# A third buffer, other slots, and ScalarE's two cross blocks moved by DMAs from its own queue

## The reference: what is computed

```python
C_q = Q @ Wq_d
C_kv = K @ Wkv_d
CqWqk = (C_q @ W_qk).reshape(b, n, H, LKV)
scores = jnp.einsum('bnhl,bkl->bhnk', CqWqk, C_kv) / jnp.sqrt(LKV)
attn = jax.nn.softmax(scores, axis=-1)
V_up = (C_kv @ Wv_u).reshape(b, nkv, H, HD)
out = jnp.einsum('bhnk,bkhd->bnhd', attn, V_up)
```

## Time and profile before

| | |
|---|---|
| median of the runs | 2763.66 us |
| the profiled execution, as timed | 2762.25 us |
| its span, first to last instruction | 2760.3 us |
| mean granted clock of TensorE | 0.985 |
| PE busy | 2608.9 us, 95% |
| DVE busy | 2311.5 us, 84% |
| POOL busy | 1938.7 us, 70% |
| ACT busy | 1687.2 us, 61% |
| blocks `b_pt<-b_tn` by DMA | 1152 of 80.0 KB, 2.8 us to landing |

### The profile page before, as it was taken

The page is one execution under the profiler, slowest core; times in us unless marked ns, Lnnn a source line. Parts: engine busy times, 40 slices in busy tenths (PEclk is TensorE's granted clock), DMA queues, the critical chain, the costliest instruction groups (busy, mean ns, idle before and its releaser), DMA issues. The chain is left out here.

```text
span 2760.3 us, 41974 instructions
## 1 busy us (share of the span) xinstructions
PE 2608.9 (95%) x14328; PEld 1983.6 (72%) x14328; DVE 2311.5 (84%) x2664; ACT 1687.2 (61%) x2636; POOL 1938.7 (70%) x1423
## 2 busy tenths in 40 slices
PE   7998899999998999999977999999999999999997
PEld 4665667666666666666656888888888888788885
DVE  2665689889998988788966999999998899899988
ACT  3454687877887778777856544445555555545553
POOL 1002377677777777677766888888887888888883
PEclk9899999999999999999998999999999999999999
DMA  7426677677778676886681222222223222232221
GB/s 274 161 96 203 213 228 216 188 231 212 224 207 260 203 212 197 250 262 207 188 280 69 84 92 100 77 72 74 69 69 130 77 84 77 69 115 77 84 93 76
DMA packets 166791, 420.63 MB, mean 152 GB/s; under 512 B 30130, under 2 KB 57652, under 8 KB 166068
## 3 DMA queue, kind: packets, MB, share of 16 engines
q1 hardware_dynamic: 164276, 409.57, 47.2%
q10 hardware_dynamic: 2304, 8.39, 0.7%
HBM read 248.43 MB, written 75.04 MB: 117 GB/s over the span
## 5 line engine op out<-in xcount | busy, mean ns | idle before, releaser
L1717 DVE SCALAR_TENSOR_TENSOR c_acc<-c_ps,c_sd,c_acc 128x1024 f32<-128x1024 f32 x448 | 573.2, 1282 | 94.6 <-PE c_ps L1564 94.4
L1622 ACT ACTIVATE c_scaled<-c_ps,c_sgu 128x1024 f32<-128x1024 f32 x336 | 375.5, 1117 | 420.7 <-PE c_ps L1564 418.8
L1294 POOL COPY b_pt<-b_tn 32x640 f32<-32x640 f32 x640 | 456.7, 714 | 240.7 <-DVE b_tn L1193 208.2
L1095 ACT ACTIVATE b_pr<-b_sc,b_nm 128x799 f32<-128x799 f32 (+1 forms) x512 | 476.3, 932 | 167.1 <-DVE b_pr L1186 154.6
L1804 POOL TENSOR_TENSOR c_sum_u<-c_sum_u,c_scaled 128x1024 f32<-128x1024 f32 x168 | 404.6, 2408 | 110.5 <-ACT c_scaled L1622 110.2
L1804 POOL TENSOR_TENSOR c_sum_g<-c_sum_g,c_scaled 128x1024 f32<-128x1024 f32 x168 | 404.8, 2410 | 81.9 <-ACT c_scaled L1622 81.6
L1032 PE MATMUL b_po<-b_pt,shared 128*64 128x256 f32 x2560 | 393.1, 395 | 45.9 <-DMA b_pt<-b_tn 44.0
L1013 PE MATMUL b_sc<-b_kh,b_qs 128*128 128x402 f32 (+1 forms) x1024 | 395.3, 386 | 19.8 <-ACT b_pr L1095 15.4
L1193 DVE STREAM_TRANSPOSE b_tn<-b_pr 128x1280 f32<-128x1280 f32 x256 | 385.5, 1506 | 12.2 <-ACT b_pr L1095 6.3
L1013 PE MATMUL b_sc<-b_kl,b_qs 128*128 128x402 f32 (+1 forms) x1024 | 356.8, 348 | 0.0
L1032 PEld LDWEIGHTS b_po<-b_pt,shared 128*64 128x64 f32 x2560 | 197.2, 138 | 196.8 <-DMA b_pt<-b_tn 70.5
(11 more groups left out here) (198 smaller groups left out, 4413.5 us busy)
## 6 DMA issues: line engine op xcount, KB each, us to landing
b_pt<-b_tn SPq DMA_DIRECT2D x1152, 80.0 KB, 2.8
c_uw_int<-wint_u SPq DMA_DIRECT2D x56, 512.0 KB, 3.5
c_gw_int<-wint_g SPq DMA_DIRECT2D x56, 512.0 KB, 3.4
c_dw_int<-wint_d SPq DMA_DIRECT2D x56, 512.0 KB, 3.5
a_cx<-in_b_ctxT SPq DMA_DIRECT2D x16, 1608.0 KB, 10.1
b_rw<-in_c_gw SPq DMA_DIRECT2D x28, 512.0 KB, 4.2
b_rz<-in_c_gz SPq DMA_DIRECT2D x28, 512.0 KB, 5.6
b_rw<-in_c_uw SPq DMA_DIRECT2D x28, 512.0 KB, 4.2
```

The lines of the kernel that those rows point to most:

```text
L1095: S.activation(pr[u % 2][:, k0:k1], sc[:, at + lo:at + hi], ACT.Exp, bias=nm[:, u % 2:u % 2 + 1], accum_out=den[:, g % 2, q, half:half + 1 ...
L1294: G.tensor_copy(pt[s][32 * c:32 * c + 32, a, :, :], tn[s][32 * a:32 * a + 32, c, :, :]).then_inc(s_block, 1)
L1622: S.activation(dst[:, :], pair[SLOT[x, t] % 4][:, :], ACT.Identity, scale=scale(x, t)).then_inc(s_e, 1)
L1717: V.scalar_tensor_tensor(out=total, in0=pair[SLOT[x, t] % 4][:, :], scalar=scale(x, t), in1=total, op0=ALU.mult, op1=ALU.add).then_inc(s_a ...
```

## The change

ACT no longer copies its two groups. It begins a DMA for each from its own queue, one in step 2p+3 and one in step 2p+4, at the end of the step; the semaphore counts DMA landings. `b_pt` gets a third buffer, in the tail of the `shared` tile, so writers wait for the weighing of pair p-3. PE weighs one step later. DVE turns before it projects and before it takes a head's output. ACT exponentiates before it casts projected queries, and copies a head's latent sum (L1116) after the first half's exponent.

As the FFN's buffers lie over `shared`, only two weight tiles are loaded early; four others follow at the end of the attention. In the FFN ACT no longer copies x into `c_acc`: the first down product is added to `c_xh`, and POOL adds `c_xl` to the sum later, once for each of the eight blocks, in the weight tiles 2, 4, ... 16.

```diff
-CN_AT = {27: (1, 0), 35: (1, 1), 75: (2, 0), 83: (2, 1), 139: (3, 0), 147: (3, 1)}
+CN_AT = {28: (1, 0), 36: (1, 1), 76: (2, 0), 84: (2, 1), 140: (3, 0), 148: (3, 1)}
-WEIGH_AT = 5
-OUT_AT = 10
+WEIGH_AT = 6
+LATENT_AT = 9
+OUT_AT = 11
+MOVES = 3
@@ attention: buffers, moved, exchange (SP)
+        pt.append(shared[:, NXC + 2 * NSZ - 8 * SEG:NXC + 2 * NSZ].rearrange("p (a z e) -> p a z e", a=4, z=2))
-            eng.wait_ge(s_cross, len(BY_SCALAR) * (p + 1))
+            eng.wait_ge(s_cross[p % 2], len(BY_SCALAR) * 16 * (p // 2 + 1))
-                if p >= 2:
-                    Q.wait_ge(s_pv, p - 1)
+                if p >= MOVES:
+                    Q.wait_ge(s_pv, p - MOVES + 1)
@@ attention: scalar
-            def cross(p):
+            def cross(p, n):
                 s = p % 2
-                S.wait_ge(s_tt, 2 * p + 2)
-                if p >= 2:
-                    S.wait_ge(s_pv, p - 1)
-                for a, c in BY_SCALAR:
-                    S.copy(pt[s][32 * c:32 * c + 32, a, :, :], tn[s][32 * a:32 * a + 32, c, :, :]).then_inc(s_cross, 1)
+                a, c = BY_SCALAR[n]
+                if n == 0:
+                    S.wait_ge(s_tt, 2 * p + 2)
+                    if p >= MOVES:
+                        S.wait_ge(s_pv, p - MOVES + 1)
+                S.dma_start(pt[p % MOVES][32 * c:32 * c + 32, a, :, :].rearrange("p t e -> p (t e)"),
+                            tn[s][32 * a:32 * a + 32, c, :, :].rearrange("p t e -> p (t e)")).then_inc(s_cross[s], 16)
             for k in range(NU + OUT_AT):
+                if k < NU:
+                    exponent(k, 1)
                 if k % 8 == 5 and k + 3 < NU:
                     project((k + 3) // 4)
-                if k < NU:
-                    exponent(k, 1)
-                if k % 4 == 0 and 8 <= k < NU + 8:
-                    out_latent(k // 4 - 2)
...
                 if k < NU:
                     exponent(k, 0)
+                if k % 4 == LATENT_AT % 4 and LATENT_AT <= k < NU + LATENT_AT:
+                    out_latent((k - LATENT_AT) // 4)
...
-                if k % 2 and 3 <= k < 2 * PAIRS + 3:
-                    cross((k - 3) // 2)
+                if 3 <= k < 2 * PAIRS + 3:
+                    cross(*divmod(k - 3, 2))
@@ attention: vector
+                if 1 <= k <= NU:
+                    turn(k - 1)
                 if k % 8 == 5 and k + 3 < NU:
                     project((k + 3) // 4)
...
-                if 1 <= k <= NU:
-                    turn(k - 1)
@@ ffn
-FIRST = [("u", 0), ("g", 0), ("u", 1), ("g", 1), ("d", 0)]
+FIRST = [("u", 0), ("g", 0)]
+SECOND = [("u", 1), ("g", 1), ("d", 0), ("d", 1)]
+LOW_AT = [2 + 2 * k for k in range(KC)]
@@ ffn: sync
-            load("d", 1)
+            for n, t in SECOND:
+                load(n, t)
@@ ffn: scalar
                 S.copy(xh[:, k, :], ps[:, :]).then_inc(s_xh, 1)
-                if f == 0:
-                    S.copy(acc[:, k, :], ps[:, :]).then_inc(s_init, 1)
@@ ffn: vector
-                total = acc[:, k, :] if n == "d" else part[n][t % 2][:, :]
+                total = before = acc[:, k, :] if n == "d" else part[n][t % 2][:, :]
                 if n == "d":
-                    if t % NI:
+                    if t == 0:
+                        V.wait_ge(s_xh, k + 1)
+                        before = xh[:, k, :].bitcast(F32)
+                    elif t == NI:
+                        V.wait_ge(s_init, KC + k + 1)
+                    elif t == LOW_AT[k] + 1:
+                        V.wait_ge(s_init, k + 1)
+                    else:
                         V.wait_ge(s_a[n], (t - 1) * KC + k + 1)
@@ ffn: gpsimd
+            def add_low(k):
+                G.wait_ge(s_a["d"], LOW_AT[k] * KC + k + 1)
+                G.wait_ge(s_xl, k + 1)
+                G.tensor_tensor(acc[:, k, :], acc[:, k, :], xl[:, k, :].bitcast(F32), ALU.add).then_inc(s_init, 1)
```

More of the change, by code:

```diff
@@ L838, in attention @@
         s_part = sem("nm_part")
-        s_move, s_block, s_cross = [sem("move0"), sem("move1")], sem("block"), sem("cross")
+        s_move, s_block, s_cross = [sem("move0"), sem("move1")], sem("block"), [sem("cross0"), sem("cross1")]
         s_tr, s_pe = sem("tr"), sem("pe")
@@ L902, in exchange @@
                 Q.wait_ge(s_tt, 2 * p + 2)
-                if p >= 2:
-                    Q.wait_ge(s_pv, p - 1)
+                if p >= MOVES:
+                    Q.wait_ge(s_pv, p - MOVES + 1)
                 for a, c in BY_DMA:
-                    Q.dma_start(pt[s][32 * c:32 * c + 32, a, :, :].rearrange("p t e -> p (t e)"),
+                    Q.dma_start(pt[p % MOVES][32 * c:32 * c + 32, a, :, :].rearrange("p t e -> p (t e)"),
                                 tn[s][32 * a:32 * a + 32, c, :, :].rearrange("p t e -> p (t e)")).then_inc(s_move[s], 16)
@@ L1028, in weigh @@
                     if t < NDT:
-                        turned = pt[s][:, :, :, 32 * t:32 * t + 32].rearrange("p a z e -> p z a e")
+                        turned = pt[p % MOVES][:, :, :, 32 * t:32 * t + 32].rearrange("p a z e -> p z a e")
                     else:
@@ L1290, in blocks @@
                 G.wait_ge(s_tt, 2 * p + 2)
-                if p >= 2:
-                    G.wait_ge(s_pv, p - 1)
+                if p >= MOVES:
+                    G.wait_ge(s_pv, p - MOVES + 1)
                 for n, (a, c) in enumerate(BY_POOL):
-                    G.tensor_copy(pt[s][32 * c:32 * c + 32, a, :, :], tn[s][32 * a:32 * a + 32, c, :, :]).then_inc(s_block, 1)
+                    G.tensor_copy(pt[p % MOVES][32 * c:32 * c + 32, a, :, :], tn[s][32 * a:32 * a + 32, c, :, :]).then_inc(s_block, 1)
                     G.wait_ge(s_block, len(BY_POOL) * p + n + 1)
@@ L1428, in ffn @@
         d1 = sb("c_dw_int1", [P, HID], F32R)
-        w = {n: [sb(f"c_{n}w_int{j}", [P, HID], F32R) for j in range(2)] for n in "gu"}
+        w = {"g": [sb("c_gw_int0", [P, HID], F32R)], "u": [sb("c_uw_int0", [P, HID], F32R)]}
+        for n in "gu":
+            w[n].append(sb(f"c_{n}w_int1", [P, HID], F32R))
         w["d"] = [sb("c_dw_int0", [P, HID], F32R), d1]
@@ L1450, in consumed @@
                 eng.wait_ge(s_xl, e[1] * KC + e[2] + 1)
-                if e[1] == 0:
-                    eng.wait_ge(s_init, e[2] + 1)
             elif e[0] == "r":
@@ L1501, in early @@
                 n = p - LATE
-                if 2 <= n < 7:
+                if 2 <= n < 2 + len(FIRST):
                     load(*FIRST[n - 2])
@@ L1716, in accumulate @@
                 V.wait_ge(s_p[n], t * KC + k + 1)
-                V.scalar_tensor_tensor(out=total, in0=pair[SLOT[x, t] % 4][:, :], scalar=scale(x, t), in1=total,
+                V.scalar_tensor_tensor(out=total, in0=pair[SLOT[x, t] % 4][:, :], scalar=scale(x, t), in1=before,
                                        op0=ALU.mult, op1=ALU.add).then_inc(s_a[n], 1)
@@ L1721, in low_turned @@
                 V.wait_ge(s_xh, f * KC + k + 1)
-                if f == 0:
-                    V.wait_ge(s_init, k + 1)
                 V.tensor_tensor(xl[:, k, :], ps[:, :], xh[:, k, :].bitcast(F32), ALU.subtract).then_inc(s_xl, 1)
@@ L1820, in low @@
                 G.tensor_tensor(hl[t % 2][:, :], h[:, :], hh[t % 2][:, :].bitcast(F32), ALU.subtract).then_inc(s_hl, 1)
+            def add_low(k):
+                G.wait_ge(s_a["d"], LOW_AT[k] * KC + k + 1)
+                G.wait_ge(s_xl, k + 1)
+                G.tensor_tensor(acc[:, k, :], acc[:, k, :], xl[:, k, :].bitcast(F32), ALU.add).then_inc(s_init, 1)
             for p, e in walk():
                 if len(e) == 2:
+                    if e[0][0] == "d" and LOW_AT[int(e[0][1])] == e[1]:
+                        add_low(int(e[0][1]))
                     if e[0] == "u0" and 0 <= p - 2 < NT2:
```

2 lines of the change are left out of this document (removed).

## The result

The changed kernel takes 2966.83 us (median of four runs, 2964.20 to 2968.39) where the kernel before takes 2762.26 beside it: 1.0723 times, 95% interval 1.0703 to 1.0743. Five executions of the experiments' kernels took far longer than the others; the ratios and intervals leave them out, the medians in us include them. The forecast was 2735, with 2795 as the far end. The last turning begins at 1636.9 us, before at 1431.7; that is 205.2 us later, and the whole span grew by 205.1 (2760.3 to 2965.4). So the feed-forward part neither won nor lost, and the attention, which now lasts to about 1640, lost everything.

What follows compares the result with a forecast made beforehand. PE (94% busy) and DVE (87%) were taken to bound the attention, so only their waits could be won. Terms -57 + 25 + 5 + 3 + 2 - 6 + 1 = -27 us gave 2735 from 2762.25; range 2685 to 2795.

Steps and rivals of the forecast that it cites:

- ACT's two blocks: DMAs replacing ACT's copies in the attention: no gain counted, 5 us lost for landings above the median; bounds 0 and 90.
- Order of the slots: DVE's projection and output behind its turning: covered by 4.31 us a step, no cost; ACT's latent sum behind an exponent: 2.
- The latent sum: ACT's latent sum behind an exponent, asked for by the next pair's weighing: 0 to 70 us over 64 heads, taken as 2.
- one of the prediction's own signs of being wrong: In the attention, PE stands at `b_po` for ACT's latent sum in more than a few heads; no size given.
- Later weighing and the third buffer: Attention: PE's wait for moved blocks goes, -57 us; DVE inherits 25 of it before its turning, between 8 and 70.5.
- Start of the FFN: ACT loses 8 copies and PE's wait for `c_xl` goes: gain 0 to 8.4 us, taken as 6.
- POOL's adds: Eight adds in the FFN, 19.3 us, fit into POOL's gaps: cost 1 us, ends 0 and 19.3.
- Traffic: 256 more DMAs of 80 KB, 21 MB or 8% more in the attention, lengthen landings: 0 to 8 us, taken as 3.
- A: Slower: ACT's queue begins the second DMA only when the exponent before it has ended; 2818 us, chance 0.14.
- its sign: DVE waits at L1193 in nearly every second unit for 0.4 us or more.
- B: No change: ACT's two issues draw out SP's nine by 0.7 us a pair; 2755 to 2774, say 2765; chance 0.25.
- B's sign: SP's issue of a block takes above 0.65 us, from 0.59.

Runs made afterwards that it cites:

- the late DMA alone: Kernel of 2753 us with only the second DMA of a pair put back behind both exponents of the even step: 2836.38 us, ratio 1.0274.
- the late reads alone: Kernel of 2753 us with only DVE's reads of projection, output and turned latent put back behind its turning: 2802.83 us, ratio 1.0137.
- every late place undone: Changed kernel with DVE's reads, ACT's cast and latent sum early again; both DMAs in the odd step: 2753.18 us (0.9951), or copies instead: 2756.46 (0.9962).
- the kernel of 2753 us: Changed kernel with both DMAs in the odd step, DVE's reads ahead of its turning, ACT's projection cast and latent sum early: 2753.18 us, ratio 0.9951.

## Why the prediction was wrong, step by step

**ACT's two blocks (+5 us): failed, the largest.** The prediction had the second DMA begin 0.64 us after the step's first exponent and land 2.0 to 2.8 later, just in time for a turning that DVE cannot want sooner than 3.50 after that exponent. The step that failed is the landing: 2.0 to 2.8 is what SP's blocks take, and the median landing was taken as what this DMA meets. With the late DMA alone it begins sooner than forecast, at 0.13, and lands 4.5 later, 5.3 beside weight transfers; DVE is ready at 3.96. The term was worth 3.2% (about 89 us) by itself, at the upper bound of 90 that the text gave it.

The program has SP issue a pair's nine blocks ahead of its weight load; what ACT begins comes later, and among the weight transfers. In the changed kernel the second DMA begins 9.7 us after the pair's turning ended (median) and meets one of these transfers in 78 of 126 pairs, two or more in 66.

In the changed kernel the begin is late as well: 1.18 us after the exponent (median of 126 pairs), held by the wait of ACT's copy, with whose start it coincides within 0.05 us in 106 of them. It lands 3.5 after that (median), so some 5.0 after the exponent (median), and DVE is ready at 4.1. The prediction read the queue from one step, in which that copy stood behind no wait that showed:

```profile
730.08 0.47 ACT L1102 COPY b_pe<-b_mi 128x384 f32<-128x384 f32 x1
```

**Order of the slots (nothing): failed.** The cover named, "wanted two steps later", looked at who wants DVE's results. It left out what DVE's reading frees. PE stands in order at its turning until the bank is read; by itself this costs 1.9%, about 51 us, with 31 waits for the projection of 1.5 us and 55 for the output of 0.4:

```profile
PE b_mi L1045 <- DVE b_qs L1176: 48.2, 31, 5.3
...
PE b_mi L1045 <- DVE b_yo L1208: 23.6, 55, 2.7
```

(from the run with the late reads alone). ACT's cast behind its exponent, which the prediction did not price either, costs 32 us where the reads are early. The latent sum, taken at 2 of a possible 70, made PE wait 26.9 us in 31 times, one of the prediction's own signs of being wrong; what that cost, 4 to 7 us by the medians, is within the noise.

**Later weighing and the third buffer (-57, and 25 back): the wait went, the gain did not.** DVE inherited nothing from SP's blocks in the changed kernel; the late ones were ACT's. But even with every late place undone, the whole is worth 0.4 to 0.5%, 10 to 14 us. In the kernel of 2753 us PE's wait for exponents grew by 30 of the 33 us that the wait for blocks gave up. Adding up an engine's waits took each as time on the path; what stands behind PE's next scores was not asked.

**Start of the FFN (-6) and POOL's adds (+1): the adds as sized, the 6 us did not come.** From the last turning's start to the end it is 1328.5 us, before 1328.6. The eight adds are there (19.3 us, nobody waits for them); PE's wait for `c_xl` over the whole part fell from 7.0 to 3.6 us, and nothing came of it.

**Traffic (+3)**: it was sized by ACT's own 21 MB; what the runs show is what these DMAs meet, which is counted above as landing.

**The rivals.** A came closest: it named DVE's turning behind ACT's DMA, the point from which it decides (landing 3.5 us after the first exponent) and 2818; the late DMA alone gave 2836. That the two agree is partly luck, since its reason was wrong: in the changed kernel the second DMA begins before the exponent ahead of it has begun in 120 of 126 pairs. Nor did its sign show as told: DVE waited in 61 of 256 turnings, not in nearly every second one. B's sign did not show: SP's issue of a block stayed at 591 ns at the median, and the 222 of SP's 1152 issues that overlap one of ACT's took 590. By the generator's lock in the Trainium skill, "Perfetto Trace Analysis", section "DMA Instruction — HWDGE (DVE, Sync)", it should have grown; at the median this trace does not agree. What ACT's DMAs do share is said in the Trainium skill, "Trainium Kernel Development and Optimization", section "Key Constraints": DMAs from all queues run on the same 16 DMA engines, and another queue saves only the time to issue. Here the trace agrees: 2.1 us to landing alone, 4.8 among the 512 KB transfers.

## What to carry to other kernels

When a read of a shared buffer is moved, ask two things: who wants its result, and who wants the place that it frees; here the second was the engine whose turn came sooner. A DMA in place of a copy has to be priced by a landing time taken from its own moment, among the transfers of that moment, and its issue can stand behind a wait that is ahead of it in the queue, as here in 106 of 126 pairs. And a wait that is removed can come back as another: here 33 us of PE's wait for blocks became 30 of its wait for exponents. So ask, before it is added to a sum, what stands next in the same round.

## What was not expected of the hardware

PE's granted clock fell after a short standstill here. Around the round shown above, in the changed kernel (columns as in the earlier trace rows):

```profile
839.00:843.00 4.00, 3.98 (x22) 2.21 (x21) 2.25 (x4) 2.36 (x6) 3.67 (x7) 1.00 0.99 324
843.00:846.00 3.00, 0.19 (x2) 0.19 (x3) 2.91 (x4) 1.89 (x4) 2.94 (x3) 1.00 0.74 146
846.00:847.40 1.40, 1.40 (x7) 0.92 (x6) 0.78 (x1) 0.48 (x1) 0.68 (x1) 0.68 0.85 328
847.40:850.60 3.20, 3.20 (x16) 1.69 (x16) 2.48 (x3) 1.02 (x2) 0.54 (x1) 0.61 0.89 343
850.60:854.00 3.40, 3.40 (x25) 3.12 (x27) 2.06 (x4) 1.40 (x3) 3.07 (x6) 1.00 0.59 147
```

PE was busy for 0.19 of 3 us, at full clock (2.4 GHz) still; in the next two stretches the mean is 0.68 and 0.61, most of the time at the lower level of 1.2 GHz; then it is 1.00 again. Such stretches are more than this one: from 338 us to the end of the attention the clock stood at the lower level in 28 stretches, 143 us in all, and in the kernel before in 6, 27 us in all.

Over the whole kernel the same 14328 matmuls kept PE busy 2663.1 us, before 2608.9: 54 of the 205 us lie in matmuls that take longer. An estimate from these rows: if PE was busy in all of the additional 116 us (143 - 27), half of it, 58 us, is lost at half the clock, about all of the 54. So this part is a price of the waits and no cause beside them. With one late part alone it is small: 12 stretches, 48 us, with the late DMA; 6 stretches, 31 us, with the late reads. It is one way in which the two together cost more than their sum.
